# Gate weight sums behind the down weight sums, the transposes of tile 30 ahead of two stores and loads, and another order of the last products

## The chip, the cores and the metric

The kernel runs on one core of one Trainium2 chip. The metric is the device time of one execution in microseconds (us), the median over runs. Engines are named as in the profile: PE is TensorE, DVE is VectorE, ACT is ScalarE, POOL is GpSimd, SP is SyncE, whose queue issues nearly all DMAs.

## What is computed

Input x is 2 x 2048 x 512. A small conditioning vector mixes eight weight matrices into one matrix per batch, x is multiplied by it and a bias is added. A gated feed-forward block follows, in which each linear layer rounds its input rows to integers and its weights to -1, 0 or 1, and the result is added to x:

```
masked_w = weight * mask[None, :, :]
w_bot = jnp.einsum('bg,got->bot', y, masked_w)
h = jnp.einsum('bnt,bot->bno', x, w_bot) + bias

wq = jnp.clip(jnp.round(w * scale), -1.0, 1.0) / scale      # scale = 1 / mean|w|
xq = jnp.clip(jnp.round(x * scale), -128.0, 127.0) / scale  # scale = 127 / max|x| of the row

gate = jax.nn.silu(_bitlinear(h, w_gate))
up = _bitlinear(h, w_up)
out = x + _bitlinear(gate * up, w_down)
```

w_gate and w_up are 2048 x 512, w_down is 512 x 2048.

## The kernel before

The 4096 rows are 32 tiles of 128 rows. There are two stages.

**The conditioning stage** walks tiles 0 to 29. PE multiplies a tile (`cond_products`, L815, f32, eight matmul records a tile), DVE adds the bias and finds the row's largest value (`cond_tile`, L632 to L640), ACT rounds it to integers (`cond_round`, L404 and L409), and SP's queue transposes it into `qT` (`transpose_q`, L217). Beside the tiles the three weights w_gate (m = 0), w_up (m = 1) and w_down (m = 2) are made ternary. ACT sums their absolute values, PE adds these over the partitions (`abs_total`, L938), DVE forms mean and inverse (`weight_mean`, L613 to L618), POOL scales the four pieces of a weight (L315), and DVE clips one piece after each of four tiles (`ternary_piece`, L623 and L625, after tiles 7 to 10, 15 to 18 and 23 to 26). DVE does `weight_mean` of w_down after tile 19, and PE waits for its first operation (L613), which empties the PSUM bank of the sum, before it starts tile 23. After tile 15 and its piece of w_up DVE computes four 16-wide columns (`units(0)`, L646 to L653).

**The feed-forward stage** walks steps s = 0 to 31, one tile each. PE computes gate and up products (`chunk`, L850 and L855), ACT the silu (L423), DVE the product (L708) and its row maximum (L726, L757), ACT rounds (L450) and converts in two halves (`convert`, L460), and SP's queue transposes each half (`transpose_q2`, L262). The down products of tiles 2j and 2j+1 are made together from seven products of half the size (`down_product(j, i)`, i = 0 to 6, L912), with sums and differences of blocks: those of the down weights are made once by POOL (`combo`, L323 to L328), those of activations by DVE (L672). Part of the gate product is grouped in the same way from step 4 on (`group_product`, L884); its weight sums `gcombo` are made once by POOL (`combine_gate`, L305 to L310). PE waits for all four `combo` before step 3 and for all four `gcombo` inside step 3, before the first `group_product`. Tiles 30 and 31 are not paired: `down_plain(t, half)` (L919) multiplies them in two halves of eight matmuls.

What sets the order: each engine works strictly in the order of its own program. SP issues DMAs in its program order, and an instruction that waits holds all that stands behind it. In step s (odd, from 5) SP stores tiles s-5 and s-4 (L268), each followed by the load of a later tile's x into `x_res` (L270), and then issues the transposes of tile s-1. The last steps hold these waits: `scale_c11(14)` on ACT (L480) needs the store of tile 26 to have landed, since it overwrites `result`; the two `convert` of tile 31 stand behind it on ACT, and need the landed transposes of tile 30; `sum_seed(14)` on DVE (L678) needs `scale_c11(14)`, and `down_product(14, 4)` needs `sum_seed(14)`.

Of the kernel before, what the change touches and what calls it, by code (L numbers as in the profile page):

```python
# [14 lines left out]
TILES = BATCH * SEQ // P  # L15
# [11 lines left out]
LATE = TILES - 2  # L27
# [24 lines left out]
def build(nc, xT, x, y_col, wcond, mask, bias, w_gate, w_up, w_down, out):  # L52
    with ExitStack() as ctx:
# [143 lines left out]
        @block.sync  # L197
        def _(sp):
            def load_xT(t):
                if t >= XSLOTS:  # L200
                    sp.wait_ge(cond_psum, t - XSLOTS + 1)
                sp.dma_start(xT_sb[:, t % XSLOTS], xT[t]).then_inc(s_xT[t % XSLOTS], 16)

            def load_mask(b, k):
                sp.dma_start(mask_sb[:, b, k], mask[b, :, k]).then_inc(s_mask[b][k], 16)

            def load_wc(k):
                for i in range(4 if k > 0 else 0):
                    sp.dma_start(wc[:, k, 2 * i:2 * i + 2], wcond[k, :, 2 * i:2 * i + 2]).then_inc(s_wc[k][i], 16)
                load_mask(0, k)  # L210

            def load_raw(m, src, a):
                sp.dma_start(raws[m][:, a], src[a]).then_inc(s_raw[m][a], 16)

            def transpose_q(t):
                sp.wait_ge(q_ready, t + 1)
                sp.dma_start_transpose(qT[:, t], q_sb[:, t % QSLOTS]).then_inc(s_qT[t % QSLOTS], 16)  # L217

            sp.dma_start(y_sb[:, :], y_col).then_inc(s_small, 16)
            load_wc(0)  # L220
            for t in range(FIRST):
                load_xT(t)
            load_wc(1)
            for t in range(FIRST, EARLY):
                load_xT(t)
            load_wc(2)
            load_wc(3)
            for t in range(EARLY, XSLOTS):
                load_xT(t)
            sp.dma_start(bias_sb[:, :], bias.partition_broadcast(P)).then_inc(s_bias, 16)  # L230
            for a in range(PIECES):
                if a % 2 == 0:
                    sp.wait_ge(mix_psum, 2 * (a // 2 + 1))
                load_raw(0, w_gate, a)
            for a in range(PIECES):
                if a % 2 == 0:
                    sp.wait_ge(mix_psum, 2 * (a // 2 + 3))
                if a == 0:
                    for t in range(XSLOTS, XSLOTS + 3):
                        load_xT(t)  # L240
                if a == 2:
                    for k in range(KH):
                        load_mask(1, k)
                    for t in range(XSLOTS + 3, AHEAD):
                        load_xT(t)
                load_raw(1, w_up, a)
            for t in range(LATE):
                if t + AHEAD < TILES:
                    load_xT(t + AHEAD)
                transpose_q(t)  # L250
                if t in (20, 21):
                    sp.dma_start(x_res[:, t - 20], x[t - 20]).then_inc(s_xres[t - 20], 16)
                if 9 <= t < 9 + PIECES:
                    sp.wait_ge(tern_done, t - 8)
                    load_raw(2, w_down, t - 9)

            def transpose_q2(t):
                if t >= QBUF:
                    sp.wait_ge(down_psum, 7 * ((t - QBUF) // 2 + 1))
                for half in range(2):  # L260
                    sp.wait_ge(q2_ready, 2 * t + half + 1)
                    sp.dma_start_transpose(q2T[:, t % QBUF, KB * half:KB * half + KB, :],  # L262
                                           q2[:, 1024 * half:1024 * half + 1024]).then_inc(s_q2T[half], 16)

            def store(t):
                par = t % 2
                sp.wait_ge(result_ready, t + 1)
                sp.dma_start(out[t], result[:, par]).then_inc(s_store[par], 16)  # L268
                if t + 2 < LATE:
                    sp.dma_start(x_res[:, par], x[t + 2]).then_inc(s_xres[par], 16)  # L270

            for s in range(1, TILES):
                if s % 2 == 1 and s >= 5:
                    store(s - 5)
                    store(s - 4)
                transpose_q2(s - 1)
                if s in (2, 3):
                    transpose_q(LATE + s - 2)
                if s == 4:
                    for q in range(QSLOTS):  # L280
                        sp.wait_ge(s_qT[q], 16 * (TILES // QSLOTS))
                    for i in range(2):
                        sp.dma_start(x_tail[:, i], x[LATE + i]).then_inc(s_xtail, 16)
            transpose_q2(TILES - 1)
            for t in (LATE - 2, LATE - 1):
                store(t)
            for i in range(2):
                sp.wait_ge(last_ready, i + 1)
                sp.dma_start(out[LATE + i], h_sb[:, i]).then_inc(s_last, 16)
            for par in range(2):  # L290
                sp.wait_ge(s_store[par], 16 * PAIRS)
            sp.wait_ge(s_last, 32)

        @block.gpsimd
        def _(pool):
# [5 lines left out]
            def combine_gate():  # L301
                b11, b12 = tern_gate[:, 2, 0:2], tern_gate[:, 3, 0:2]
                b21, b22 = tern_gate[:, 2, 2:4], tern_gate[:, 3, 2:4]
                pool.wait_ge(tern_done, PIECES)
                nc.gpsimd.tensor_tensor(gcombo[:, 0], b12, b11, ALU.subtract).then_inc(gcombo_ready, 1)  # L305
                nc.gpsimd.tensor_tensor(gcombo[:, 2], b22, b12, ALU.subtract).then_inc(gcombo_ready, 1)
                pool.wait_ge(gcombo_ready, 1)
                nc.gpsimd.tensor_tensor(gcombo[:, 1], b22, gcombo[:, 0], ALU.subtract).then_inc(gcombo_ready, 1)
                pool.wait_ge(gcombo_ready, 3)
                nc.gpsimd.tensor_tensor(gcombo[:, 3], b21, gcombo[:, 1], ALU.subtract).then_inc(gcombo_ready, 1)  # L310

            for m in range(3):
                pool.wait_ge(mean_step, 3 * (m + 1))
                for a in range(PIECES):
                    nc.gpsimd.tensor_scalar(raws[m][:, a], raws[m][:, a], w_inv[:, m:m + 1], ROUND, ALU.mult, ALU.add  # L315
                                            ).then_inc(scaled, 1)
                if m == 1:
                    combine_gate()

            b11, b12 = tern_down[:, 0:KB, 0:NB], tern_down[:, 0:KB, NB:HID]  # L320
            b21, b22 = tern_down[:, KB:KI, 0:NB], tern_down[:, KB:KI, NB:HID]
# [4 lines left out]
            nc.gpsimd.tensor_tensor(combo[:, 1], b22, combo[:, 0], ALU.subtract).then_inc(combo_ready, 1)  # L326
            pool.wait_ge(combo_ready, 3)
            nc.gpsimd.tensor_tensor(combo[:, 3], b21, combo[:, 1], ALU.subtract).then_inc(combo_ready, 1)  # L328

            def unit_of(t):  # L330
                pool.wait_ge(p_col, 3 * t + 1)
                nc.gpsimd.tensor_scalar(out_unit[:, t:t + 1], p_max[:, t % 2:t % 2 + 1], up_step[:, t:t + 1], w_mean[:, 2:3],  # L332
                                        ALU.mult, ALU.mult).then_inc(unit_done, 1)
# [478 lines left out]
        def _(pe):  # L812
# [103 lines left out]
            def down_plain(t, half):  # L916
                pe.wait_ge(s_q2T[half], 16 * t + 16)
                for k in range(KB * half, KB * half + KB):
                    ins = nc.tensor.matmul(ps[:, LAST[t - LATE]], q2T[:, t % QBUF, k], tern_down[:, k], start=(k == 0),  # L919
                                           stop=(k == KI - 1))  # L920
                if half == 1:
                    ins.then_inc(plain_psum, 1)
# [83 lines left out]
                step(s, s % 2, (s - 4 + s % 2) // 2, (s - 4 + s % 2) % QBUF, g if s < TILES - 1 else None, g % 2)  # L1006
            b0 = (LATE - 2) % QBUF
            down_product(PAIRS - 1, 2, b0, b0 + 1)
            down_plain(LATE, 0)
            down_product(PAIRS - 1, 3, b0, b0 + 1)  # L1010
            down_plain(LATE, 1)
            down_product(PAIRS - 1, 4, b0, b0 + 1)
            down_product(PAIRS - 1, 5, b0, b0 + 1)
            down_plain(LATE + 1, 0)
# [40 lines left out]
```

## Time and profile before

| | |
|---|---|
| median of 3 runs | 468.85 us (468.77 to 468.87) |
| profiled execution, its own time | 469.65 us |
| span in the profile | 467.9 us |
| PE busy | 444.7 us (95%) |
| DVE busy | 350.6 us (75%) |
| ACT busy | 320.0 us (68%) |
| POOL busy | 151.6 us (32%) |
| mean granted PE clock | 0.984 |

The span runs from the first to the last instruction; 1.75 us of the profiled execution lie outside it. A granted clock of 1.00 is 2.4 GHz, 0.50 is 1.2 GHz. PE is busy almost everywhere, so what matters are the few places where it waits and the stretches at the lower clock.

### The profile page before, as it was taken

How to read it: one execution, taken by the hardware profiler on the slowest of the kernel's cores; microseconds unless marked ns; L12 is line 12 of the kernel's file. 1: busy time of each engine (PE TensorE's matmuls, PEld its weight loads, DVE VectorE, ACT ScalarE, POOL GpSimd, SP SyncE). 2: the span in 40 equal slices, each digit the busy share in tenths (PEclk: the TensorE clock that was granted, in tenths of full speed). 3: DMA queues.
4: the chain of work that ended last, by engine and by line, in shares of the span. 5: the costliest groups of instructions: out<-in, count | busy, mean ns of one | idle time of the engine just before them, and what ended most of it. 6: DMA issues, size and time to landing. Idle time of an engine off the chain costs nothing.

```text
span 467.9 us, 7111 instructions
## 1 busy us (share of the span) xinstructions
PE 444.7 (95%) x2194; PEld 235.4 (50%) x2194; DVE 350.6 (75%) x600; ACT 320.0 (68%) x424; POOL 151.6 (32%) x160
## 2 busy tenths in 40 slices
PE   4899998985999999999999999999999999999976
PEld 0234443432444456555565555655556555565533
DVE  0315779898965799788887888878888788887842
ACT  1216766845345798978879788797887978879730
POOL 0000351935086113341433414334143341432302
PEclk9999999997999999999999999999999999999979
DMA  8999996962710245434655345433454334543382
GB/s 286 405 399 415 405 222 193 381 158 45 146 34 13 45 87 122 131 92 112 125 124 92 90 112 144 102 90 90 112 144 103 90 90 112 144 102 91 92 136 90
DMA packets 104313, 69.78 MB, mean 149 GB/s; under 512 B 87264, under 2 KB 87264, under 8 KB 102752
## 3 DMA queue, kind: packets, MB, share of 16 engines
q1 hardware_dynamic: 103712, 67.39, 53.2%
q10 hardware_dynamic: 576, 2.10, 1.2%
q8 instruction: 10, 0.16, 0.1%
q14 instruction: 15, 0.12, 0.1%
HBM read 40.11 MB, written 8.39 MB: 104 GB/s over the span
## 4 chain that ended last, share of the span: by engine, by line
PE 78%; DMA 9%; DVE 5%; ACT 3%; issue 2%; POOL 2%; ACTq 0%; SPq 0%; DVEq 0%
PE ps L855 24%; PE ps L912 19%; PE ps L850 13%; PE ps L884 9%; PE ps L815 9%; DMA wc<-w_gate 4%; DMA qT<-q_sb 3%; PE ps L919 2%; PE ps L828 2%; POOL wc L315 2%; DMA wc<-wcond 1%; DVE tern_up L623 1%; DMA wc<-wc 1%; ACT tern_up L398 1%; DVE h_max L634 1%
## 5 line engine op out<-in xcount | busy, mean ns | idle before, releaser
L855 PE MATMUL ps<-tern_up,qT 128*128 128x512 f16 x512 | 131.4, 379 | 0.0
L815 PE MATMUL ps<-w_bot,xT_sb 128*128 128x512 f32 x256 | 115.9, 606 | 8.4 <-DVE w_mean L613 6.8
L815 PEld LDWEIGHTS ps<-w_bot,xT_sb 128*128 128x128 f32 x256 | 48.9, 194 | 69.2 <-issue 65.5
L726 DVE TENSOR_REDUCE p_part<-wc 128x1 f32<-128x1536 f32 x64 | 77.9, 1217 | 1.7
L855 PEld LDWEIGHTS ps<-tern_up,qT 128*128 (+1 forms) x512 | 50.1, 98 | 54.2
L708 DVE TENSOR_TENSOR wc<-ps,wc 128x512 f32<-128x512 f32 x72 | 49.6, 690 | 36.6 <-PE ps L855 34.4
L850 PE MATMUL ps<-tern_gate,qT 128*128 128x512 f16 x288 | 73.9, 379 | 0.0
L460 ACT ACTIVATE wc<-wc 128x1024 f16<-128x1024 f32 x64 | 67.2, 1053 | 2.5 <-DMA wc<-wc 2.5
L912 PE MATMUL ps<-wc 128*128 128x256 f16 x480 | 63.1, 275 | 0.0
L450 ACT ACTIVATE wc<-wc,p_scale 128x2048 f32<-128x2048 f32 x31 | 61.7, 1991 | 0.0
L423 ACT ACTIVATE wc<-ps,gate_unit 128x512 f32<-128x512 f32 x72 | 49.4, 687 | 16.8 <-PE ps L850 16.6
L912 PEld LDWEIGHTS ps<-wc 128*128 128x128 f16 x480 | 47.4, 99 | 18.6 <-issue 0.5
L446 ACT ACTIVATE w_bot<-ps,gate_unit 128x512 f32<-128x512 f32 x42 | 28.8, 687 | 36.1 <-PE ps L884 35.2
L315 POOL TENSOR_SCALAR wc<-wc,w_inv 128x2048 f32<-128x2048 f32 x12 | 25.3, 2129 | 81.3 <-DVE w_inv L618 81.3
L339 POOL TENSOR_TENSOR result<-result,x_res 128x512 f32<-128x512 f32 x15 | 19.1, 1271 | 100.1 <-issue 100.1
L912 PE MATMUL ps<-tern_down,wc 128*128 128x256 f16 x360 | 46.7, 273 | 0.5 <-ACT ps L473 0.5
L850 PEld LDWEIGHTS ps<-tern_gate,qT 128*128 (+1 forms) x288 | 28.2, 98 | 37.0 <-issue 5.0
L672 DVE TENSOR_TENSOR wc<-wc 128x1024 f16<-128x1024 f16 x60 | 44.5, 742 | 0.1
L332 POOL TENSOR_SCALAR out_unit<-p_max,up_step,w_mean 128x1 f32<-128x1 f32 x32 | 10.9, 340 | 99.9 <-DVE p_max L757 99.9
L912 PEld LDWEIGHTS ps<-tern_down,wc 128*128 128x128 f16 x360 | 35.1, 98 | 14.2 <-ACT ps L473 0.7
L404 ACT ACTIVATE h_sb<-h_sb,h_inv 128x512 f32<-128x512 f32 x32 | 22.9, 715 | 27.0 <-DVE h_inv L640 27.0
L708 DVE TENSOR_TENSOR wc<-ps,w_bot 128x512 f32<-128x512 f32 x56 | 38.4, 685 | 2.4 <-PE ps L855 2.0
(83 smaller groups left out, 473.7 us busy)
## 6 DMA issues: line engine op xcount, KB each, us to landing
xT_sb<-xT SPq DMA_DIRECT2D x32, 256.0 KB, 7.1
x_res<-x SPq DMA_DIRECT2D x30, 256.0 KB, 3.0
out<-result SPq DMA_DIRECT2D x30, 256.0 KB, 2.1
wc<-wcond SPq DMA_DIRECT2D x12, 512.0 KB, 13.5
wc<-w_gate SPq DMA_DIRECT2D x4, 1024.0 KB, 17.3
wc<-w_up SPq DMA_DIRECT2D x4, 1024.0 KB, 13.1
wc<-w_down SPq DMA_DIRECT2D x4, 1024.0 KB, 7.3
wc<-wcond ACTq DMA_DIRECT2D x4, 512.0 KB, 7.7
```

Source lines behind the costliest of these rows:

```text
L315: nc.gpsimd.tensor_scalar(raws[m][:, a], raws[m][:, a], w_inv[:, m:m + 1], ROUND, ALU.mult, ALU.add).then_inc(scaled, 1)
L423: nc.scalar.activation(silu[:, n % 2], ps[:, GATE + n % 2], ACT.Silu, scale=unit_column(s)).then_inc(silu_ready, 1)
L450: nc.scalar.activation(prod[:, par], prod[:, par], ACT.Copy, bias=ROUND, scale=p_scale[:, par:par + 1]).then_inc(p_rounded, 1)
L460: nc.scalar.activation(q2[:, 1024 * half:1024 * half + 1024], prod[:, par, 1024 * half:1024 * half + 1024], ACT.Copy, bias=-ROUND).then_in ...
L672: nc.vector.tensor_tensor(qsum[:, i], in0, in1, op).then_inc(sum_ready, 1)
L708: nc.vector.tensor_tensor(prod[:, par, 512 * c:512 * c + 512], ps[:, UP + i % 2], source, ALU.mult).then_inc(prod_ready, 1)
L726: nc.vector.tensor_reduce(p_part[:, par, i:i + 1], prod[:, par, 512 * lo:512 * hi], AX.X, ALU.max, apply_absolute_value=True).then_inc(par ...
L815: ins = nc.tensor.matmul(ps[:, t % COND_BANKS], xT_sb[:, t % XSLOTS, k], w_bot[:, t // HALF, k], start=(k == 0), stop=(k == KH - 1))
L850: ins = nc.tensor.matmul(ps[:, bank], tile_of(s, k), tern_gate[:, c, k], start=(k == 0), stop=(k == KH - 1))
L855: ins = nc.tensor.matmul(ps[:, UP + i % 2], tile_of(s, k), tern_up[:, c, k], start=(k == 0), stop=(k == KH - 1))
L884: ins = nc.tensor.matmul(ps[:, bank], tile, weight, start=(i < 2 and k == 0), stop=(k == 1), skip_group_check=(i >= 2))
L912: ins = nc.tensor.matmul(ps[:, bank, 0:NB], tile, weight, start=(i < 2 and k == 0), stop=(k == KB - 1), skip_group_check=(i >= 2))
```

## The change

Three edits, in the program's own lines:

```diff
@@ SP
             for s in range(1, TILES):
+                if s == TILES - 1:
+                    transpose_q2(s - 1)
                 if s % 2 == 1 and s >= 5:
                     store(s - 5)
                     store(s - 4)
-                transpose_q2(s - 1)
+                if s < TILES - 1:
+                    transpose_q2(s - 1)
@@ POOL
                 for a in range(PIECES):
                     nc.gpsimd.tensor_scalar(raws[m][:, a], raws[m][:, a], w_inv[:, m:m + 1], ROUND, ALU.mult, ALU.add
                                             ).then_inc(scaled, 1)
-                if m == 1:
-                    combine_gate()
...
             nc.gpsimd.tensor_tensor(combo[:, 3], b21, combo[:, 1], ALU.subtract).then_inc(combo_ready, 1)
+            combine_gate()
@@ PE
             down_product(PAIRS - 1, 2, b0, b0 + 1)
-            down_plain(LATE, 0)
             down_product(PAIRS - 1, 3, b0, b0 + 1)
-            down_plain(LATE, 1)
+            for half in range(2):
+                down_plain(LATE, half)
             down_product(PAIRS - 1, 4, b0, b0 + 1)
```

POOL, from the scaling of w_up on, before. `wc` holds the raw weights and `combo`:

```order
12 L315 TENSOR_SCALAR wc<-wc,w_inv 128x2048 [waits mean_step]
13 L315 TENSOR_SCALAR wc<-wc,w_inv 128x2048 x3
14 L305 TENSOR_TENSOR gcombo<-tern_gate 128x1024 [waits tern_done]
15 L306 TENSOR_TENSOR gcombo<-tern_gate 128x1024
16 L308 TENSOR_TENSOR gcombo<-tern_gate,gcombo 128x1024 [waits gcombo_ready]
17 L310 TENSOR_TENSOR gcombo<-tern_gate,gcombo 128x1024 [waits gcombo_ready]
18 L315 TENSOR_SCALAR wc<-wc,w_inv 128x2048 [waits mean_step]
19 L315 TENSOR_SCALAR wc<-wc,w_inv 128x2048 x3
20 L323 TENSOR_TENSOR wc<-tern_down 128x2048 [waits tern_done]
21 L324 TENSOR_TENSOR wc<-tern_down 128x2048
22 L326 TENSOR_TENSOR wc<-tern_down,wc 128x2048 [waits combo_ready]
23 L328 TENSOR_TENSOR wc<-tern_down,wc 128x2048 [waits combo_ready]
```

POOL at the same place after:

```order
14 L318 TENSOR_SCALAR wc<-wc,w_inv 128x2048 [waits mean_step]
15 L318 TENSOR_SCALAR wc<-wc,w_inv 128x2048 x3
16 L324 TENSOR_TENSOR wc<-tern_down 128x2048 [waits tern_done]
17 L325 TENSOR_TENSOR wc<-tern_down 128x2048
18 L327 TENSOR_TENSOR wc<-tern_down,wc 128x2048 [waits combo_ready]
19 L329 TENSOR_TENSOR wc<-tern_down,wc 128x2048 [waits combo_ready]
20 L308 TENSOR_TENSOR gcombo<-tern_gate 128x1024 [waits tern_done]
21 L309 TENSOR_TENSOR gcombo<-tern_gate 128x1024
22 L311 TENSOR_TENSOR gcombo<-tern_gate,gcombo 128x1024 [waits gcombo_ready]
23 L313 TENSOR_TENSOR gcombo<-tern_gate,gcombo 128x1024 [waits gcombo_ready]
24 L334 TENSOR_SCALAR out_unit<-p_max,up_step,w_mean 128x1 [waits p_col] x2
```

The four sums of gate weights moved from between the scaling of w_up and that of w_down to the end of the weight work, ahead of the first `unit_of` of the feed-forward stage.

SP's queue at the end, before. The transposes of `wc` are those of tile 30 and then tile 31, two halves each:

```order
183 L268 DMA out<-result 128x512 [waits result_ready]
184 L270 DMA x_res<-x 128x512
185 L268 DMA out<-result 128x512 [waits result_ready]
186 L270 DMA x_res<-x 128x512
187 L262 DMA_TRANSPOSE wc<-wc 128x8x128 [waits q2_ready,down_psum]
188 L262 DMA_TRANSPOSE wc<-wc 128x8x128 [waits q2_ready]
189 L262 DMA_TRANSPOSE wc<-wc 128x8x128 [waits q2_ready,down_psum]
190 L262 DMA_TRANSPOSE wc<-wc 128x8x128 [waits q2_ready]
```

and after:

```order
183 L262 DMA_TRANSPOSE wc<-wc 128x8x128 [waits q2_ready,down_psum]
184 L262 DMA_TRANSPOSE wc<-wc 128x8x128 [waits q2_ready]
185 L268 DMA out<-result 128x512 [waits result_ready]
186 L270 DMA x_res<-x 128x512
187 L268 DMA out<-result 128x512 [waits result_ready]
188 L270 DMA x_res<-x 128x512
189 L262 DMA_TRANSPOSE wc<-wc 128x8x128 [waits q2_ready,down_psum]
190 L262 DMA_TRANSPOSE wc<-wc 128x8x128 [waits q2_ready]
```

Both transposes of tile 30 now stand ahead of the stores of tiles 26 and 27 and the loads of x of tiles 28 and 29.

PE behind the last step, before:

```order
534 L912 MATMUL ps<-tern_down,wc 128x256 [waits s_q2T1,seed_copied]
535 L912 MATMUL ps<-tern_down,wc 128x256 x7
536 L919 MATMUL ps<-tern_down,wc 128x512 [waits s_q2T0]
537 L919 MATMUL ps<-tern_down,wc 128x512 x7
538 L912 MATMUL ps<-wc 128x256 [waits sum_ready]
539 L912 MATMUL ps<-wc 128x256 x7
540 L919 MATMUL ps<-tern_down,wc 128x512 [waits s_q2T1]
541 L919 MATMUL ps<-tern_down,wc 128x512 x7
542 L912 MATMUL ps<-tern_down,wc 128x256 [waits sum_ready,seed_summed]
```

and after:

```order
534 L914 MATMUL ps<-tern_down,wc 128x256 [waits s_q2T1,seed_copied]
535 L914 MATMUL ps<-tern_down,wc 128x256 x7
536 L914 MATMUL ps<-wc 128x256 [waits sum_ready]
537 L914 MATMUL ps<-wc 128x256 x7
538 L921 MATMUL ps<-tern_down,wc 128x512 [waits s_q2T0]
539 L921 MATMUL ps<-tern_down,wc 128x512 x7
540 L921 MATMUL ps<-tern_down,wc 128x512 [waits s_q2T1]
541 L921 MATMUL ps<-tern_down,wc 128x512 x7
542 L914 MATMUL ps<-tern_down,wc 128x256 [waits sum_ready,seed_summed]
```

`down_product(14, 3)`, which waits for no transpose of tile 30, moved ahead of both halves of `down_plain(30)`. The rest is in the same order.

## Rows read from the trace of the kernel before

**Rows 1.** Waits: engine, line, whom it waited for: us in total, times, longest.

```profile
PE ps L815 <- DVE w_mean L613: 6.8, 2, 6.2
```

**Rows 2.** Timeline of PE: start, us, engine, line, operation, count, idle before.

```profile
79.33 17.41 PE L815 MATMUL ps<-w_bot,xT_sb 128*128 128x512 f32 x40 [0.64 <-DVE w_mean L613]
...
109.98 26.71 PE L815 MATMUL ps<-w_bot,xT_sb 128*128 128x512 f32 x56 [6.16 <-DVE w_mean L613]
136.53 1.03 PE L850 MATMUL ps<-tern_gate,qT 128*128 128x512 f16 x4
```

**Rows 3.** Windows: stretch, us, busy time by engine, granted PE clock, DMA share, GB/s.

```profile
108.00:110.00 2.00, 0.02 (x1) 0.05 (x1) 1.86 (x7) 0.19 (x1) 0.00 (x0) 0.52 0.32 66
```

**Rows 4.** Timeline of DVE in the conditioning stage.

```profile
87.50 3.14 DVE L623 TENSOR_SCALAR tern_up<-wc 128x2048 f16<-128x2048 f32 x1 [1.08 <-POOL wc L315]
...
97.32 0.68 DVE L632 TENSOR_TENSOR h_sb<-ps,bias_sb 128x512 f32<-128x512 f32 x1
...
109.69 0.14 DVE L613 TENSOR_REDUCE w_mean<-ps 128x1 f32<-128x4 f32 x1
```

**Rows 5.** Instructions of single lines: duration in ns min/median/max, first and last start.

```profile
L623 DVE TENSOR_SCALAR tern_up<-wc x4: 1207/1208/3139, 87.5 to 106.1; 128x2048 f16<-128x2048 f32 x4
L625 DVE TENSOR_SCALAR tern_up<-tern_up x4: 693/694/2506, 90.7 to 107.4; 128x2048 f16<-128x2048 f16 x4
L646 DVE TENSOR_SCALAR gate_unit<-h_unit,w_mean x2: 233/1164/2094, 93.1 to 175.7; 128x16 f32<-128x16 f32 x2
```

**Rows 6.** Timeline of POOL: first and last sum of gate weights, last of down weights.

```profile
87.44 2.12 POOL L305 TENSOR_TENSOR gcombo<-tern_gate 128x1024 f16<-128x1024 f16 x1
...
95.25 2.12 POOL L310 TENSOR_TENSOR gcombo<-tern_gate,gcombo 128x1024 f16<-128x1024 f16 x1
...
143.07 4.07 POOL L328 TENSOR_TENSOR wc<-tern_down,wc 128x2048 f16<-128x2048 f16 x1
```

**Rows 7.** Timeline of DVE, and of PE, in steps 0 and 3.

```profile
146.67 0.27 DVE L757 TENSOR_SCALAR p_max<-p_part,p_floor 128x1 f32<-128x1 f32 x1
...
167.57 0.59 PE L884 MATMUL ps<-gcombo,w_bot 128*128 128x512 f16 x2
```

**Rows 8.** Timeline of SP's queue at the end.

```profile
444.09 0.34 SPq L268 DMA_DIRECT2D out<-result  x1
...
445.00 9.17 SPq L262 DMA_TRANSPOSE wc<-wc  x4
```

**Rows 9.** Line L262: time from issue to landing, all 64 transposes.

```profile
DMA to landing us min/median/max: 3.0/3.1/5.3
```

**Rows 10.** DMA of 447 to 448: queue, packets, MB, share; then of 230 to 233.

```profile
q8 instruction: 1, 0.02, 5.9%
...
q8 instruction: 1, 0.02, 1.9%
...
wc<-wc SPq DMA_TRANSPOSE x2, 5.1
```

**Rows 11.** Timeline of all engines at the end.

```profile
443.01 1.05 ACT L460 ACTIVATE wc<-wc 128x1024 f16<-128x1024 f32 x1
...
444.44 1.05 ACT L460 ACTIVATE wc<-wc 128x1024 f16<-128x1024 f32 x1
...
446.32 1.05 PE L912 MATMUL ps<-tern_down,wc 128*128 128x256 f16 x8 [0.46 <-ACT ps L473]
...
447.41 0.47 ACT L480 ACTIVATE result<-ps,out_unit 128x256 f32<-128x256 f32 x1 [1.14 <-PE ps L912]
...
450.39 3.60 PE L919 MATMUL ps<-tern_down,wc 128*128 128x512 f16 x8 [3.02 <-DMA wc<-wc]
450.43 2.00 ACT L460 ACTIVATE wc<-wc 128x1024 f16<-128x1024 f32 x2 [2.55 <-DMA wc<-wc]
...
461.93 1.89 PE L919 MATMUL ps<-tern_down,wc 128*128 128x512 f16 x8
```

**Rows 12.** Window of the end in which the granted clock fell.

```profile
449.00:450.00 1.00, 0.00 (x0) 0.00 (x0) 0.37 (x1) 0.00 (x0) 0.00 (x0) 0.70 0.89 195
```

## The prediction

> **What bounds the kernel now.** I read the page first (PE is busy nearly always), then the waits, then the timelines around the two places where PE stops. The first stop is in the conditioning stage: PE waits 6.2 us once for DVE's `w_mean` [rows 1]. The timeline of PE shows what follows: 56 matmul records from 109.98 to 136.53, 26.55 us or 0.474 us each. The 40 records from 79.33 at full clock take 17.24 us up to the next operation, which starts 0.17 us before they are counted as ended, so 0.431 us each [rows 2]. The granted clock is 0.52 in the two us before PE restarts [rows 3]: the idle time brought PE down to the lower of its two levels, 1.2 GHz, and it begins the 56 records there. From 136.53 to 446 PE is never idle for long, so a shift there arrives at the end whole. The second stop is at the end: PE finishes `down_product(14, 2)` at 447.37, waits 3.02 us for the first transpose of tile 30, and then runs `down_plain(30, 0)` at 0.45 us a matmul; the last eight of the same shape take 1.89 us together [rows 11]. The clock fell again inside that wait [rows 12].
>
> **Edit 1, the sums of gate weights, at the old place.** The four sums occupy POOL from 87.44 to 97.37, 9.93 us [rows 6]. In exactly that time DVE's clipping takes 3.14 and 2.51 us, where the same instructions take 1.21 and 0.69 otherwise, and the first column operation takes 2.09 us against 0.23 [rows 4, 5]. DVE starts tile 16 at 97.32, as POOL ends. Without POOL beside it: 87.50 + 1.21 + 0.69 = 89.4, and four column operations at about 0.25 us each (the one undisturbed row says 0.23) give 90.4. DVE comes 97.3 - 90.4 = 6.9 us earlier to tile 16, and 6.9 us earlier to `w_mean`: 109.69 - 6.9 = 102.8 [rows 4]. PE wants to go on at 109.98 - 6.16 = 103.8 [rows 2], some 1 us later than that. The whole wait goes: **6.2 us**. Without it the 56 records keep the full clock: 26.55 - 56 x 0.431 = **2.4 us**. Sum 8.6 us. The margin of 1 us is thin. If DVE came only 4 us earlier, the wait would shrink by 4 and the clock would probably hold, which gives 6 instead of 8.6. The other ends of this term: nothing, if something else slows DVE there, and 8.6, since PE's own matmuls then bound. I take 8.6 because the row that decides, DVE restarting as POOL ends, leaves no second cause needed.
>
> What is late next? DVE's later tiles, POOL's scaling of w_down and the clipping all hang on `w_mean`, and come 6.9 us earlier in a row; PE comes 8.6 us earlier, so DVE loses 1.7 us of slack against PE. In the old trace DVE waits for PE in tiles 28 and 29, so this slack exists.
>
> The Trainium skill, SBUF — State Buffer, section Who interferes with whom, says that GpSimd and VectorE share a pair of ports as an exclusive lock, taken by a `tensor_scalar` in a two-port mode or by an operation with two SBUF inputs against a GpSimd read. By that rule the slow rows are blocked rows and the whole excess goes; the trace agrees, with 3.14 against 1.21 us [rows 5].
>
> **Edit 1, at the new place.** The down sums end at 147.14 [rows 6] and begin once DVE has clipped w_down, which comes 6.9 us earlier, so 140.2. The gate sums then take between 4 x 2.12 = 8.5 (the unhindered row) and 9.93 us: done by 148.7 to 150.1. PE needs them at 167.57 - 8.6 = 159.0 [rows 7]. The cover is 9 us; beyond it each us of POOL costs PE one. `unit_of(0)` and `unit_of(1)` stand behind them on POOL; DVE asks for the first when it writes `p_max` of step 2, 8 us after the sums end. What can DVE lose? In steps 0 and 1 it does products with one input in PSUM, reductions and one-wide columns. Such work already ran beside the down sums: the `p_max` operation took 0.27 us inside a POOL sum [rows 6, 7]. I cost it at nothing; upper bound 4 x (2.09 - 0.23) = 7.4 us, if all four sums caught such an operation as L646 was caught.
>
> **Edit 2, transposes of tile 30 first.** ACT's first `convert` of tile 30 is done at 444.06, the second at 445.49 [rows 11]. Before, SP then stores tile 27 at 444.09, loads x, and issues the first transpose at 445.00 [rows 8]. It lands after 5.3 us, at 450.3, the slowest of all; the usual is 3.0 to 3.1 [rows 9]. Now it is issued at 444.1, 0.9 us earlier. I expect it to land at 444.1 + 3.1 = 447.2. The second is issued at 445.5.
>
> Why 5.3 us? An instruction fetch is on the DMA engines at 447 to 448 [rows 10], and a second one, at 230 to 233, has transposes of 5.1 us beside it. Fetches that fell before the transposes were under way left them at the usual 3.1, so it is the overlap that counts. The fetch depends on PE's place in its program, which the edit does not change up to there, so I keep it at that time. The first transpose would be through before it, the second would be hit and land at about 445.5 + 3.1 + 1.5 = 450.1 (a share of the excess of 2.2 us).
>
> **A new wait takes over.** The store of tile 26 had been issued long before; now it stands behind both transposes of tile 30. `scale_c11(14)` on ACT needs it landed, and behind that on ACT are the two `convert` of tile 31. Free of a stall the store goes out at 446.8 and lands at about 449.3; behind a second transpose that lands at 450.1, it lands at about 450.7. Then 0.47 for `scale_c11`, 1.05 for `convert`, 0.1 for issue and 3.1 to landing [rows 9, 11]: the first transpose of tile 31 is there at 455.4, and PE can start `down_plain(31, 0)` then. The loads of x behind the stores are wanted only by POOL's last additions, later.
>
> **Edit 3, the order of PE.** At full clock `down_product` takes 0.87 us and a half of `down_plain` 1.73 (the 1.89 us of the last row less the pipelined tail). `down_product(14, 3)` fills 447.4 to 448.2 of the old idle time. `down_plain(30, 0)` runs to 450.0, half 1 from 450.1 to 451.9; `sum_seed` on DVE needs `scale_c11`, so products 4 and 5 end by 454.0; wait to 455.4; `down_plain(31, 0)`, product 6, `down_plain(31, 1)`: 1.73 + 0.87 + 1.73 = 4.35, end 459.8. Before it was 461.93 + 1.89 = 463.8 [rows 11]. **Gain 4.0 us.** What follows the last matmul (last addition, store) is unchanged.
>
> **Sum.** 8.6 + 4.0 = 12.6 us off the profiled execution: 469.65 - 12.6 = 457.05. The median of the runs lies 0.8 us below the profiled execution, so 468.85 - 12.6 = **456.2 us**.
>
> **Rivals.**
> (a) No stall at the end. The store of tile 26 lands at 449.3, everything of tile 31 comes 1.4 us earlier, gain 5.4 there: 454.8. For: the excess has been seen on a few transposes only, and timing is close. Against: both overlaps in rows 10 came with the excess. The Trainium skill, Runtime: NRT & Kernel Launch, section Instruction fetch mechanics, calls the cost of crossing a block of instructions mostly hidden; by that the fetch delays nothing and this rival is the outcome. The trace speaks against it with the 5.1 and 5.3 us.
> (b) The clock falls at the end after all. PE still waits some 1.4 us for tile 31. In the old trace it had been idle for about 2 us when the clock fell [rows 11, 12], after 6.2 us the other time [rows 3]. If it falls, the last 16 large and 8 small matmuls take up to twice 4.35 us and the gain of the end is gone: 460.3.
> (c) The wait for `w_mean` shrinks only in part, because DVE is held by something else in tiles 16 to 19: gain 6 or less there, 458.8 or more, 464.9 if nothing goes.
> (d) Slower. The slow clipping at 87.5 has another cause, so the old place gives nothing, and at the new place POOL's sums block DVE's small operations in steps 0 and 1, where PE waits for each product: up to 7.4 us. It decides from the point where this exceeds the 4.0 us of the end: 468.85 - 4.0 + 7.4 = 472.3. Against it stand the undisturbed 0.27 us and that DVE restarts just as POOL ends.
> (e) The change doesn't do what it says: the transposes of tile 30 wait anyway for product 6 of pair 13 or ACT. ACT ends at 444.06 and that product ended before; then only the first term remains, 460.2.
>
> **How the numbers follow.** Forecast 0.47; (a) 0.21; (b) 0.10; (c) 0.12; (d) 0.03; (e) 0.03; nothing to be measured 0.04. From 454.0 (rival (a) with 0.8 us to spare) to 459.5 (the forecast with the transposes of tile 31 later by 3.3 us, or most of (c)) the range holds the first two and about two thirds of (c), near 0.8 with a little of (b). A difference below 0.2%, 0.9 us, can't be told from none. Faster 0.94, same 0.03, slower 0.03.
>
> **What would show it.** `w_mean` L613 at 102.8 and no PE wait above 1 us there; clock 1.00 through the conditioning stage; clipping at 1.21 us throughout; the first L884 at about 159; at the end no wait of 3 us before `down_plain(30, 0)`, but one of 1 to 2 us before `down_plain(31, 0)`, with ACT's `scale_c11` held by the DMA of `result`. Wrong would be: DVE still slow at 87.5, a wait for `gcombo`, or a clock of 0.50 after 440.

## The result

The changed kernel takes 457.16 us in the median of 4 runs (456.83 to 457.30), the kernel before 468.86 (468.77 to 469.17). The ratio is 0.9748, with a 95% interval of 0.9731 to 0.9765: 11.7 us or 2.5% faster. The profiled execution went from 469.65 to 457.30 us, its span from 467.9 to 455.5. The forecast was 456.2 us, with a range of 454.0 to 459.5.

The head of the page of the changed kernel:

```profile
span 455.5 us, 7111 instructions
...
PE 439.4 (96%) x2194; PEld 233.7 (51%) x2194; DVE 343.1 (75%) x600; ACT 319.7 (70%) x424; POOL 150.8 (33%) x160
...
PEclk9999999999999999999999999999999999999999
```

The granted clock is now at nine tenths or more in all 40 slices, where the page before shows two at seven. PE is busy 5.3 us less, with the same matmuls: that is what ran at the lower clock before.

The timeline of PE in the conditioning stage, to be held against [rows 2]:

```profile
79.53 17.41 PE L817 MATMUL ps<-w_bot,xT_sb 128*128 128x512 f32 x40 [0.64 <-DVE w_mean L615]
97.19 0.36 PE L940 MATMUL ps<-abs_sum,ones 128*128 128x4 f32 x2 [0.26 <-ACT tern_down L400]
97.41 31.15 PE L817 MATMUL ps<-w_bot,xT_sb 128*128 128x512 f32 x72
128.39 1.03 PE L852 MATMUL ps<-tern_gate,qT 128*128 128x512 f16 x4
```

The 16 and the 56 records are now one row of 72: the wait of 6.16 us is gone, and the first gate product comes at 128.39 instead of 136.53, 8.1 us earlier. DVE shows why, against [rows 4, 5]:

```profile
87.73 1.23 DVE L625 TENSOR_SCALAR tern_up<-wc 128x2048 f16<-128x2048 f32 x1 [1.11 <-POOL wc L318]
88.99 0.69 DVE L627 TENSOR_SCALAR tern_up<-tern_up 128x2048 f16<-128x2048 f16 x1
89.60 0.23 DVE L648 TENSOR_SCALAR gate_unit<-h_unit,w_mean 128x16 f32<-128x16 f32 x1
...
90.37 0.69 DVE L634 TENSOR_TENSOR h_sb<-ps,bias_sb 128x512 f32<-128x512 f32 x1
...
102.76 0.14 DVE L615 TENSOR_REDUCE w_mean<-ps 128x1 f32<-128x4 f32 x1
```

The clipping takes 1.23 and 0.69 us instead of 3.14 and 2.51, tile 16 starts at 90.37 instead of 97.32, and `w_mean` comes at 102.76. POOL's last gate sum, against [rows 6], and PE's first use of it, against [rows 7]:

```profile
146.56 2.13 POOL L313 TENSOR_TENSOR gcombo<-tern_gate,gcombo 128x1024 f16<-128x1024 f16 x1
...
159.43 0.59 PE L886 MATMUL ps<-gcombo,w_bot 128*128 128x512 f16 x2
```

The end of the program on PE, ACT and SP, against [rows 8, 11]:

```profile
436.00 3.41 SPq L262 DMA_TRANSPOSE wc<-wc  x2
...
438.19 1.05 PE L914 MATMUL ps<-tern_down,wc 128*128 128x256 f16 x8 [0.46 <-ACT ps L475]
...
439.45 0.58 SPq L268 DMA_DIRECT2D out<-result  x1
...
440.47 3.63 PE L921 MATMUL ps<-tern_down,wc 128*128 128x512 f16 x16 [0.36 <-DMA wc<-wc]
...
442.22 0.47 ACT L482 ACTIVATE result<-ps,out_unit 128x256 f32<-128x256 f32 x1 [4.09 <-DMA out<-result]
442.59 1.99 ACT L462 ACTIVATE wc<-wc 128x1024 f16<-128x1024 f32 x2
...
443.71 2.62 SPq L262 DMA_TRANSPOSE wc<-wc  x2
...
446.97 1.90 PE L921 MATMUL ps<-tern_down,wc 128*128 128x512 f16 x8 [1.07 <-DMA wc<-wc]
...
449.75 1.74 PE ps L921 x8
```

(The last line is from the chain that ended last.) The wait before `down_plain(30)` is 0.36 us instead of 3.02, and both halves run at full clock. ACT waits 4.09 us for the landing of the store of tile 26, tile 31's transposes start only behind that, and PE waits 1.07 us before `down_plain(31)`. From the start of `down_product(14, 2)` to the last matmul's end the program takes 451.49 - 438.19 = 13.3 us, and 463.8 - 446.32 = 17.5 us before: 4.2 us. Below, "the end" means this stretch.

### The profile page after: what moved, and what is told of

Same layout as the page of the kernel before. It is cut to its first block, busy times and chain, and to the rows that moved or that the text cites. A ratio compares the mean times of both kernels' runs of the same rounds, so it can differ in the third digit from the quotient of the medians.

```text
span 455.5 us, 7111 instructions
## 1 busy us (share of the span) xinstructions
PE 439.4 (96%) x2194; PEld 233.7 (51%) x2194; DVE 343.1 (75%) x600; ACT 319.7 (70%) x424; POOL 150.8 (33%) x160
## 4 chain that ended last, share of the span: by engine, by line
PE 78%; DMA 13%; ACT 3%; SPq 2%; issue 1%; DVE 1%; ACTq 0%; DVEq 0%
PE ps L857 24%; PE ps L914 19%; PE ps L852 14%; PE ps L817 10%; PE ps L886 9%; DMA wc<-w_gate 4%; DMA qT<-q_sb 3%; DMA wc<-wcond 2%; DMA wc<-w_down 2%; PE ps L830 1%; ACT tern_up L400 1%; SPq L217 1%; ACT h_sb L406 1%; PE ps L921 1%; DMA wc<-wc 1%
## 5 line engine op out<-in xcount | busy, mean ns | idle before, releaser
L817 PE MATMUL ps<-w_bot,xT_sb 128*128 128x512 f32 x256 | 113.2, 595 | 2.3 <-DVE w_bot L611 1.6
```

The lines of the kernel that those rows point to most:

```text
L817: ins = nc.tensor.matmul(ps[:, t % COND_BANKS], xT_sb[:, t % XSLOTS, k], w_bot[:, t // HALF, k], start=(k == 0), stop=(k == KH - 1))
```

## The experiments

Ten kernels and two repetitions ran, in three groups, all on chips on which the kernel before had a wider spread than above: 465.4 to 470.7 us in 29 runs beside the first group, median 468.99, and 469.34 and 469.35 beside the other two. I therefore take times as good to about 1 us, and the traces carry the finer statements; each run has one trace.

### Each edit by itself

**Edit 1 alone.** The POOL part of the diff, nothing else.

> Edit 1 alone, from the kernel before. If the sums of gate weights beside DVE's clipping were what made PE wait, the whole gain of the conditioning stage is here: the first L850 comes 8.1 us earlier (128.4 instead of 136.5), the clipping takes 1.21 us, and the median is 468.9 - 8.1 = 460.8 us (460.3 to 461.3). The rival, that something else slowed DVE, gives 468.9. The end of the program should look as before, with a first transpose of tile 30 of about 5 us, a PE wait of 3 us and a clock of 0.50 behind it.

Measured: 461.03 us, ratio 0.9831 (0.9792 to 0.987). The first gate product comes at 128.81. The end is that of before, here in the timeline of PE and the windows (granted clock third from the right):

```profile
438.60 1.05 PE L911 MATMUL ps<-tern_down,wc 128*128 128x256 f16 x8 [0.46 <-ACT ps L472]
442.56 3.59 PE L918 MATMUL ps<-tern_down,wc 128*128 128x512 f16 x8 [2.91 <-DMA wc<-wc]
...
442.00:443.00 1.00, 0.44 (x2) 0.17 (x3) 0.00 (x0) 0.41 (x1) 0.00 (x0) 0.50 1.08 243
```

The end takes 17.2 us here. The whole gain of the conditioning stage belongs to edit 1. The six runs of this kernel differ in the clock granted over the span: three at 0.991 take 461.2 to 461.9 us, two at 0.994 and 0.996 take 460.8 and 459.7, and the one at 1.000 takes 458.7. Only one of them was traced, at 461.67 us with the clock down at the end. That the others differ by whether and how long the clock falls there is my reading of these means, not shown; by it the fall costs some 3 us.

**Edit 2 alone.** The SP part of the diff.

> Edit 2 alone, from the kernel before, with PE's old order of the last products. My reading of the end is that the landing of tile 31's first transpose bounds it, set by the store of tile 26. Then PE's order hardly matters: the wait before down_plain(30, 0) is about 1 us instead of 3, the clock stays at 1.00, and the gain is nearly the whole 4.2 us: 464.9 us (464.4 to 465.6). If the order of the products carries the gain, this gives 467 or more, with the clock at 0.50 at the end.

Measured: 466.18 us, ratio 0.9944 (0.9917 to 0.997), 1.3 us above what I expected. The trace has the effect nearly whole:

```profile
446.69 1.05 PE L915 MATMUL ps<-tern_down,wc 128*128 128x256 f16 x8 [0.46 <-ACT ps L476]
...
449.31 1.90 PE L922 MATMUL ps<-tern_down,wc 128*128 128x512 f16 x8 [1.57 <-DMA wc<-wc]
...
458.43 1.89 PE L922 MATMUL ps<-tern_down,wc 128*128 128x512 f16 x8
```

The wait is 1.57 us, the clock stays at 1.00, and the end takes 13.6 us, 3.9 less than before. The medians differ by 2.8 us only. Part of the difference can lie in the conditioning stage, which none of the edits at the end touches and which still varies: the first gate product comes at 136.90 here, at 135.66 in the trace of edit 3 alone, at 136.14 in that of both, and at 136.53 before. The rest is open.

**Edit 3 alone.** The PE part of the diff.

> Edit 3 alone, from the kernel before. down_product(14, 3) fills 0.9 us of the 3.0 us wait, which leaves 2.1 us. If the clock holds over that, the rest runs at full clock and the end comes 3.9 us earlier: 465.0. If the clock falls as before, only the 0.9 us moved is hidden and the slow stretch is the same: 468.0 to 468.9. I hold the fall for the likelier, since in the kernel before the clock had fallen 2 us into the wait.

Measured: 465.87 us, ratio 0.9945 (0.9923 to 0.9968). The likelier of my two cases was the wrong one:

```profile
445.45 1.05 PE L912 MATMUL ps<-tern_down,wc 128*128 128x256 f16 x8 [0.46 <-ACT ps L473]
446.33 1.04 PE L912 MATMUL ps<-wc 128*128 128x256 f16 x8
...
449.34 3.63 PE L919 MATMUL ps<-tern_down,wc 128*128 128x512 f16 x16 [1.97 <-DMA wc<-wc]
...
457.15 1.89 PE L919 MATMUL ps<-tern_down,wc 128*128 128x512 f16 x8
```

The transposes are as late as before, but the wait is 1.97 us, the clock holds, and the end takes 13.6 us. So either edit alone gives 3.9 us in the trace: both do the same thing, they make the stop so short that the clock held in these traces. What the clock is worth can be read off: the two halves of `down_plain(30)` and `down_product(14, 3)` took 457.58 - 450.39 = 7.2 us before; here the two halves take 452.81 - 449.34 = 3.5 us and the product 0.9, so 2.8 us of the gain is clock and 0.9 the product that now fills the wait.

**Edits 2 and 3 together.**

> Edits 2 and 3 without edit 1. If the two places are independent, this gains the 4.2 us of the end and nothing in the conditioning stage: 464.6 us, and the gains of edit 1 alone and of this add up to the whole change within 0.5 us.

Measured: 465.66 us, ratio 0.9935 (0.9913 to 0.9957). The end takes 459.23 - 445.94 = 13.3 us, as in the changed kernel. The second of the two edits adds 0.3 us. Against the kernel before beside them, edit 1 gains 8.0 us and these two 3.3, 11.3 together, where the whole change gained 11.7: the two places are independent, as far as times good to 1 us can say.

### The sums of gate weights

**Half of them at the old place.** In the changed kernel, `combine_gate` is cut in two:

```diff
+                if m == 1:
+                    combine_gate(0)      # gcombo 0 and 2
...
-            combine_gate()
+            combine_gate(1)              # gcombo 1 and 3
```

> The changed kernel, but with two of the four gate sums back at the old place. Theory: DVE is blocked only while a sum runs. Two sums take about 5 us there, so DVE's first clipping is slow (3.1 us) and the second in part, DVE loses about 2.7 us instead of 7, w_mean comes at about 105.5, and PE, which would go on at 104.3, waits 1.0 to 1.5 us at a clock that holds: 457.2 + 1.2 = 458.4 us. If the loss were in proportion to the sums moved, half of 8.1 us would be back: 461.2. If the gate sums did not matter: 457.2.

Measured: 460.81 us, ratio 0.9825 (0.9784 to 0.9867), 3.2 to 3.7 us above the changed kernel, and not the 1.2 expected. The timelines of DVE and PE and a window:

```profile
88.02 3.14 DVE L629 TENSOR_SCALAR tern_up<-wc 128x2048 f16<-128x2048 f32 x1 [1.10 <-POOL wc L320]
91.20 2.50 DVE L631 TENSOR_SCALAR tern_up<-tern_up 128x2048 f16<-128x2048 f16 x1
93.62 0.22 DVE L652 TENSOR_SCALAR gate_unit<-h_unit,w_mean 128x16 f32<-128x16 f32 x1
...
107.06 25.97 PE L821 MATMUL ps<-w_bot,xT_sb 128*128 128x512 f32 x56 [2.42 <-DVE w_mean L619]
...
108.00:110.00 2.00, 2.00 (x4) 0.96 (x3) 1.90 (x5) 1.20 (x3) 2.00 (x2) 0.50 0.04 8
```

POOL's two sums end at 93.15. Each of DVE's two clippings falls onto one of them, and the column operations behind are free again, at 0.22 us instead of 2.09. DVE is slow exactly while a gate sum runs; that is the cause, shown. The blocking goes both ways: the first sum takes 2.13 us, but the second starts at 90.04, while DVE's first clipping still runs, to 91.16, and takes 3.11. I had sized it wrongly: the two sums cost DVE 3.7 us (3.14 and 2.50 against 1.23 and 0.69), not 2.7, since the second clipping too is held until its sum ends. And with PE's wait of 2.42 us the clock went down, 0.9 us after PE was back at work, which costs another 1.7 us (132.86 - 107.06 = 25.8 against 24.1 for 56 records). The Trainium skill, SBUF — State Buffer, section Who interferes with whom, has the loser block fully until the other's instruction ends; the 2.50 us here, for an instruction of 0.69, agree.

**Later than their cover.** Eight further sums of the same size ahead of the four, one waiting for another:

```diff
+            for n in range(8):
+                nc.gpsimd.tensor_tensor(gcombo[:, 3], tern_gate[:, 2, 0:2], tern_gate[:, 3, 0:2], ALU.subtract
+                                        ).then_inc(extra_sum, 1)
+                pool.wait_ge(extra_sum, n + 1)
             combine_gate()
```

> The changed kernel with eight further sums of the gate weights' size on POOL, ahead of the four, which puts these 17 us later: done at 166 instead of 148.7. The cover was 10.8 us (PE needs them at 159.4), so it is gone. Theory: POOL's next work, the unit of step 0 and the first block sums of activations, is late too; PE waits for about 8 us in step 3 and restarts at the lower clock, which costs 2 to 3 more: 467 to 468.5 us. If the sums had a looser deadline than PE's wait in step 3: under 460.

Measured: 468.09 us, ratio 0.9979 (0.9958 to 1.0).

```profile
168.35 1.01 PE L891 MATMUL ps<-gcombo,w_bot 128*128 128x512 f16 x2 [7.82 <-POOL w_bot L376]
...
168.00:170.00 2.00, 1.65 (x4) 0.58 (x5) 2.00 (x3) 2.00 (x2) 1.92 (x4) 0.50 0.00 0
```

PE waits 7.82 us and restarts at the lower clock. The last gate sum ends at 166.93; what PE waits for last is the first block sum of activations (`add_tiles`), which stands behind the gate sums on POOL. This is the price if the cover is gone: 10.5 us above the changed kernel beside it (457.62), more than the 8.0 that edit 1 gained.

### The transposes and the fetch of instructions

**A shift of PE's program, from the kernel before.** The profile shows fetches of instructions as queue q8, ten of 16 KB over the span. 16 tiny matmuls at PE's start, where it waits for the first weights, put all that follows further back in PE's program, so that a fetch for PE comes at another time:

```diff
+            pe.wait_ge(ident_ready, 1)
+            for _ in range(16):
+                nc.tensor.matmul(ps[:, 7, 0:4], ident[:, :], ident[:, 0:4], start=True, stop=True)
             pe.wait_ge(mix_w_ready, 3)
```

> The kernel before with 16 tiny matmuls (128x4) added on PE at its start, while PE waits for the first weights. They cost no time themselves and push each later instruction of PE 32 instructions back in its program, so that fetches of instructions come 2 to 3 us earlier. Theory: the first transpose of tile 30 lands after 5.3 us because a fetch falls into it. Then here it lands after 3.1 to 3.3 us, PE waits about 1 us instead of 3, the clock holds, and the time is about 464.5 us. Rival: the loads and stores just ahead of the transposes delay it, whatever the fetch does: 5.3 us and 468.9 as before.

Measured: 465.51 us, ratio 0.9919 (0.9896 to 0.9943). The fetch on q8 that fell at 447 is at 442 here, 5 us earlier and not 2 to 3. Line L262 in the window of the first transpose of tile 30, then the timeline of PE:

```profile
DMA to landing us min/median/max: 3.4/3.4/3.4
...
446.37 1.05 PE L912 MATMUL ps<-tern_down,wc 128*128 128x256 f16 x8 [0.46 <-ACT ps L473]
...
448.44 1.90 PE L919 MATMUL ps<-tern_down,wc 128*128 128x512 f16 x8 [1.02 <-DMA wc<-wc]
...
457.12 1.89 PE L919 MATMUL ps<-tern_down,wc 128*128 128x512 f16 x8
```

The landing takes 3.4 us instead of 5.3, behind the same store and load; PE waits 1.02 us, the clock holds, and the end takes 12.6 us, 4.9 less. In the trace this does more than edits 2 and 3. It changes nothing in the order of transfers: store, load and transpose are issued at 444.13, 444.51 and 445.04, where they were at 444.09, 444.47 and 445.00. So the fetch, not the transfers ahead, made the transpose slow; 1.9 of the 2.2 us above the usual 3.1 went with it.

**The same shift in the changed kernel.**

> The changed kernel with the 16 tiny matmuls of the fetch experiment. If the fetch is what delays the transposes of tile 30 there (4.4 and 3.9 us), they land after 3.1 us, the store of tile 26 goes out at 438.6 instead of 439.5 and lands at 440.9 instead of 442.1, and everything of tile 31 comes 1.2 us earlier: 456.0 us. If the fetch has no part: 457.2.

Measured: 457.63 us, ratio 0.9773 (0.9734 to 0.9812). In the trace the fetch is at 434.5, ahead of the transposes of tile 30, which land after 3.3 and 3.1 us (4.4 and 3.9 before the shift), ACT waits 3.1 us for the store instead of 4.09, and the end takes 12.3 us instead of 13.3. The traced execution took 456.59 us, the other three 457.5 to 458.8, so the median does not show it. A place that costs some executions 1 us and more is met below; that it hides the gain here is not shown.

### The store in front

**The store of tile 26 left ahead of the transposes**, with the load behind it; only tile 27's pair stands behind them:

```diff
             for s in range(1, TILES):
+                if s % 2 == 1 and s >= 5:
+                    store(s - 5)
                 if s == TILES - 1:
                     transpose_q2(s - 1)
                 if s % 2 == 1 and s >= 5:
-                    store(s - 5)
                     store(s - 4)
```

> The changed kernel, but with the store of tile 26 and the load behind it left ahead of the transposes of tile 30; only the store of tile 27 and its load stand behind them. Theory: in the changed kernel ACT waits 4.1 us for the store of tile 26, and tile 31's transposes are late by that. Here scale_c11 runs at its old time, the convert of tile 31 starts when the first transpose of tile 30 has landed (about 440.4 in the changed kernel's time, instead of 442.6), its transpose lands about 2.0 us earlier, and PE is bound by its own matmuls and by the second transpose of tile 30: a gain of 1.1 us, 456.1 us. If the store did not matter: 457.2.

Measured: 456.20 us, ratio 0.9733 (0.9695 to 0.977). The end takes 12.2 us in the trace. The traced execution was the slowest of the four, 457.45 us: PE waits 1.33 us before its sum of the absolute values of w_down, at 98.42, and the clock holds. Run again beside the changed kernel, on one chip:

> The changed kernel once more, as the yardstick of this group on the same chip. 457.2 us, with the first half of down_plain(30) held for the transpose of tile 30 by less than 1 us and that of tile 31 by about 1.1 us.

> The kernel with the store of tile 26 left in front, again, beside the changed kernel. By its trace PE needs 12.2 us from the start of down_product(14, 2) to the end of its last matmul, where the changed kernel needs 13.3: a gain of 1.1 us, 456.1 us. If the store's landing were no real bound, no difference.

Measured: the changed kernel 457.62 us (457.33 to 459.68), this one 456.97 (456.32 to 460.06), 6 runs each. Its timeline:

```profile
438.39 1.05 PE L915 MATMUL ps<-tern_down,wc 128*128 128x256 f16 x8 [0.46 <-ACT ps L476]
...
439.47 0.47 ACT L483 ACTIVATE result<-ps,out_unit 128x256 f32<-128x256 f32 x1 [1.14 <-PE ps L915]
440.84 2.00 ACT L463 ACTIVATE wc<-wc 128x1024 f16<-128x1024 f32 x2 [0.89 <-DVE wc L772]
...
446.01 1.89 PE L922 MATMUL ps<-tern_down,wc 128*128 128x512 f16 x8
...
448.61 1.89 PE L922 MATMUL ps<-tern_down,wc 128*128 128x512 f16 x8
```

ACT's wait for the store is gone, `down_plain(31)` starts without a wait, and the end takes 12.1 us instead of 13.4 in the trace of the changed kernel beside it (451.69 - 438.25). The new wait of the changed kernel is shown, and it is worth 1.3 us in the trace. The medians differ by 0.65 us, in that direction, which the spread of these runs can't tell from none.

**Both, store in front and shift.**

> The changed kernel with the store of tile 26 left in front and the 16 tiny matmuls at PE's start. Each of the two has shown about 1 us of the end by itself. Theory: with no store to wait for and no fetch across the transposes, nothing holds PE from down_product(14, 3) on, and its products take 0.87 x 4 + 1.73 x 4 = 10.4 us plus 0.9 us in front: 11.4 instead of 13.3 us, 455.3 us. Rival: both remove the same wait, and together they give what one gives, 456.1.

Measured: 458.54 us (455.79 to 459.82), ratio 0.976 (0.9726 to 0.9793): no faster, against both of my cases. The end takes 453.24 - 441.79 = 11.45 us, as the theory said. But this execution lost time far from there:

```profile
98.74 0.35 PE L944 MATMUL ps<-abs_sum,ones 128*128 128x4 f32 x2 [1.93 <-ACT tern_down L401]
...
100.00:102.00 2.00, 2.00 (x3) 0.67 (x2) 1.93 (x4) 1.94 (x4) 0.00 (x0) 0.50 0.73 202
```

PE waits 1.93 us for the absolute sums of w_down, whose second piece of four landed late and with it the rest (ACT's longest wait for a piece is 2.3 us here, 0.9 in the changed kernel's first trace), and 0.6 us after it is back at work the clock falls. The runs fall into two parts: 455.8 and 456.4 with a clock of 1.000, and 459.1 to 459.8 with 0.996, one more at 458.0 with 1.000. That the load of w_down makes this difference is read from this trace and the milder one above (1.33 us, clock held); no run changed that load, so why it is late in some executions stays open.

## Why the prediction was right

**The sum.** On the profiled execution 12.6 us were forecast and 12.35 came. The first term was 8.6 and measured 8.1, the second 4.0 and measured 4.2. The forecast median was 1.0 us too low; 0.25 of this is the sum, and the rest is that I carried the 0.8 us between profiled execution and median over to the changed kernel, where it is 0.14.

**Edit 1, old place.** Each step is in the trace: clipping at its undisturbed durations, tile 16 at 90.37 (forecast 90.4), `w_mean` at 102.76 (102.8), no wait of PE for it, full clock. The missing 0.5 us is at a place that I did not look at: PE's sum of absolute values now starts at 97.19 instead of 96.57. Of these 0.6 us, 0.2 were there before the edit acts (79.53 against 79.33), and the rest is the landing of w_down. By the starts of the rows PE would have gone on at 96.71 + 16 x 0.431 = 103.6, not 103.8, so the term should have read 8.8, and 0.7 is missing (the row behind the sum starts at 97.41 instead of 96.71). Before, such a delay was hidden behind the later wait for `w_mean`; now PE is the bound there and it counts. Edit 1 does not cause it: the traces of edit 3 alone and of edits 2 and 3 have PE waiting 0.32 and 0.63 us at the same place. The 2.4 us for the clock are one trace's too. Without edit 1 the 56 records took 26.8 us with edit 2, 25.6 with edit 3 and 25.8 with both, so the price lies between 1.5 and 2.7 us, and that it was 2.4 in the profiled execution is chance. I said that with DVE only 4 us earlier the clock would probably hold, for a gain of 6 (4 + 2.4 is 6.4). That would have left PE a wait of 2.2 us, and no run has it: the clock held after 1.97 and fell with 2.42, and in another run with 1.93. And in rival (b) I misread rows 3: the mean of 0.52 from 108 to 110 means that the clock had fallen by 108.1, some 4 us into the first wait, not after 6.2.

**Edit 1, new place.** The sums take 2.12 or 2.13 us each, as in the unhindered row, and are done at 148.69; PE needs them at 159.43. DVE's products with one input in PSUM take 0.69 us beside them and its `p_max` operation 0.27, as elsewhere. The cost is nothing, as said. Rivals (c) and (d) are out, and the run with late sums shows what it costs when the cover is used up.

**Edits 2 and 3.** The total is right, the parts less so, and that they cancel is luck. The first transpose of tile 30 did not escape the fetch: it took 4.4 us, not 3.1, and the second 3.9, not 4.6. I had kept the fetch at its time, 447.6 in the old trace; it came at 438.0, which is 446.1 there. It comes earlier in the trace of edit 2 alone as well, at 446.6 with `down_product(14, 2)` at 446.69, and not in that of edit 3 alone, at 446.5 with the product at 445.45. So edit 2 moved it against PE's work; how, no run shows. The store of tile 26 went out at 439.45 and landed after 2.7 us, at 442.1; in the old trace's time (8.1 us later) that is 450.3, where I had 450.7. From there the chain is as written down: the wait for tile 31's first transpose, 1.07 us instead of 1.4, and the end. Rival (a) is out in this kernel, but what it assumed is real: move the fetch and the end takes 1 us less. Rival (b), the clock falling at the end, did not occur, and (e) is out, since tile 30's transposes were issued first as planned. What I had not seen is that 2.8 of the 4 us were the clock's, and that each of edit 2, edit 3 and a shift of PE's program gets them alone.

## What to carry to other kernels

Work on GpSimd that nobody waits for is not free where it blocks DVE: look at DVE's durations beside it, line by line, and put it where they stay as they are, as DVE's products from PSUM and its reductions did here. Where PE stops, price the stretch behind the stop as well; a stop that becomes 1 or 2 us shorter can be worth more than its own length. When a transfer is moved ahead, follow what it overtakes: the store that fell behind was waited for by ACT, and ACT held the next tile.

## What the runs showed of the hardware

- A fetch of instructions that falls into DMA transposes in flight delays them: 5.3 us to landing before, 3.4 with the fetch moved by 16 tiny matmuls, at the same order of transfers; in the changed kernel 4.4 and 3.9, and 3.3 and 3.1 with the fetch moved. The trace of before has another case, with a fetch at 252.7 and transposes issued at 250.0 and 251.6 that took 5.2 and 4.3 us. The Trainium skill, Runtime: NRT & Kernel Launch, section Instruction fetch mechanics, calls the cost of crossing a block mostly hidden; here it was worth up to 4.9 us, through PE's wait and clock.
- A stop of PE of about 2 us can go either way. The clock stayed at 2.4 GHz with stops of 1.02, 1.07, 1.33, 1.57 and 1.97 us; with one of 1.93 us in another place it fell to 1.2 GHz, 0.6 us after PE was back at work, and with one of 2.42 us 0.9 us after. In both traces with a stop of 2.9 or 3.0 us at the end it fell during the stop, 1.6 to 2 us into it. A fall cost 1.5 to 2.8 us where it could be read off.
- GpSimd's sums and DVE's clipping block each other in turn: a clipping of 1.23 us took 3.14 and one of 0.69 took 2.50 beside sums, and the sum that began under a clipping took 3.11 us instead of 2.13. DVE's reductions, its one-column operations and its products from PSUM kept their durations beside the same sums.
